# Late butterfly weights loaded group by group, outer weights and bias packed by partition, and the rows of ones written first

## The reference, cut to what matters

```python
def butterfly(y, weights, dim):
    for stage in range(weights.shape[0]):
        s = 2 ** stage
        nb = dim // (2 * s)
        yr = y.reshape(*lead, nb, 2, s)
        a, b = yr[..., 0, :], yr[..., 1, :]
        w = weights[stage].reshape(nb, s, 2, 2)
        na = w[..., 0, 0] * a + w[..., 0, 1] * b
        nb2 = w[..., 1, 0] * a + w[..., 1, 1] * b
        y = jnp.stack([na, nb2], axis=-2).reshape(*lead, dim)
    return y
...
h = jnp.einsum('bsd,dh->bsh', x, W_exp) + b_exp
h = butterfly(h, up_weights, D_HIDDEN)
h = jax.nn.gelu(h + up_bias, approximate=False)
h = butterfly(h, down_weights, D_HIDDEN)
y = jnp.einsum('bsh,hd->bsd', h, W_con) + b_con
return y + down_bias
...
x = x + 0.5 * ffn(layernorm(x))
x = x + attn(layernorm(x))
x = x + 0.5 * ffn(layernorm(x))
```

## Time and profile before

| | |
|---|---|
| median of 3 runs | 2010.09 us (2008.09 to 2011.85) |
| profiled execution, its own time | 2014.8 us |
| span of its trace | 2013.0 us |
| TensorE busy in the span | 1953.7 us (97%) |
| VectorE, ScalarE, GpSimd busy | 1675.2, 1362.5, 306.0 us |
| TensorE's mean granted clock | 0.991 of full speed |

### The profile page before, as it was taken

How to read it: one execution, slowest core, us unless ns; L and a number is a source line. 1 busy time by engine, 2 the same in 40 slices (tenths; PEclk the granted TensorE clock), 3 DMA queues, 4 the chain that set the end, 5 groups by cost and what they waited for, 6 DMA issues and landing times.

```text
span 2013.0 us, 58994 instructions
## 1 busy us (share of the span) xinstructions
PE 1953.7 (97%) x24312; PEld 1200.6 (60%) x24312; DVE 1675.2 (83%) x3622; ACT 1362.5 (68%) x1642; POOL 306.0 (15%) x736
## 2 busy tenths in 40 slices
PE   2899999999999999999999999999999999999999
PEld 2787777655555555555555555555555555569998
DVE  5745666599999999999999999999999999847663
ACT  4521222378888888888888888888888888884444
POOL 1200000011111111111111111111111111124444
PEclk8999999899999999999999999999999999999999
DMA  4221112121121111111111211112111111101110
GB/s 125 71 98 51 50 52 88 67 49 42 39 53 40 48 45 44 42 39 53 40 48 45 44 43 39 53 40 47 45 44 43 39 53 32 61 28 63 55 51 22
DMA packets 85736, 102.20 MB, mean 51 GB/s; under 512 B 19676, under 2 KB 48092, under 8 KB 85468
## 3 DMA queue, kind: packets, MB, share of 16 engines
q1 hardware_dynamic: 85048, 98.08, 17.5%
q10 hardware_dynamic: 420, 0.34, 0.1%
HBM read 68.46 MB, written 29.36 MB: 49 GB/s over the span
## 4 chain that ended last, share of the span: by engine, by line
PE 91%; DVE 3%; issue 2%; SPq 1%; ACT 1%; POOL 1%; DMA 1%; POOLq 0%; ACTq 0%; DVEq 0%
PE PS L1145 32%; PE PS L1272 32%; PE PS L1122 7%; PE PS L1092 6%; PE PS L1252 6%; PE PS L1331 4%; PE PS L1197 2%; PE PS L1116 1%; PE PS L1058 1%; SPq L382 1%; DMA V<-down_w 1%; ACT PG L707 1%; DVE OA L805 1%; POOL QT L573 0%; DVE OA L910 0%
## 5 line engine op out<-in xcount | busy, mean ns | idle before, releaser
L707 ACT ACTIVATE PG<-PS 128x1024 f32<-128x1024 f32 (+1 forms) x1152 | 1117.2, 978 | 235.4 <-PE PS L1252 175.9
L934 DVE TENSOR_REDUCE MXP<-PS 128x1 f32<-128x512 f32 x1792 | 1099.9, 684 | 23.3 <-PE PS L1145 23.2
L1252 PE MATMUL PS<-QT,KT 50*128 50x512 f32 (+1 forms) x2304 | 803.8, 435 | 0.2 <-issue 0.2
L1145 PE MATMUL PS<-KT,QT 48*128 48x512 f32 (+3 forms) x2304 | 798.7, 432 | 2.6 <-DVE MXP L934 2.3
L1272 PE MATMUL PS<-PG,VH 128*17 128x128 f32 x16896 | 728.8, 276 | 0.2
L1272 PEld LDWEIGHTS PS<-PG,VH 128*17 128x17 f32 x16896 | 401.1, 97 | 413.7 <-issue 364.6
L1145 PEld LDWEIGHTS PS<-KT,QT 48*128 48x128 f32 x2304 | 340.7, 185 | 252.4 <-issue 141.6
L1252 PEld LDWEIGHTS PS<-QT,KT 50*128 50x128 f32 x2304 | 335.6, 185 | 10.5 <-issue 10.1
L930 DVE CUSTOM_DVE_ANT_0 PS<-PS,MASK 128x128 f32<-128x128 f32 (+3 forms) x512 | 248.8, 505 | 72.8 <-PE PS L1145 67.0
L553 POOL TENSOR_SCALAR_AFFINE_SELECT PG<-PG 128x128 f32<-128x128 f32 x512 | 137.2, 295 | 998.1 <-ACT PG L707 997.8
L631 ACT ACTIVATE PG<-PS,GB 128x512 f32<-128x512 f32 x128 | 90.3, 707 | 167.7 <-PE PS L1092 167.7
(11 more groups left out here) (111 smaller groups left out, 1201.8 us busy)
## 6 DMA issues: line engine op xcount, KB each, us to landing
QT<-q_parts SPq DMA_DIRECT2D x256, 64.0 KB
KT<-k_parts SPq DMA_DIRECT2D x256, 64.0 KB
q_parts<-OA SPq DMA_DIRECT2D x16, 512.0 KB, 2.8
QT<-q_parts SPq DMA_DIRECT2D x256, 32.0 KB
k_parts<-OA SPq DMA_DIRECT2D x16, 512.0 KB, 4.5
KT<-k_parts SPq DMA_DIRECT2D x256, 32.0 KB
o_parts<-OS SPq DMA_DIRECT2D x128, 64.0 KB
OA<-o_parts SPq DMA_DIRECT2D x32, 256.0 KB
```

The costliest lines, as they stand in the source:

```text
L707: nc.scalar.activation(PB[n % 2][half][:, :, q0:TILE], PS[:, half * 1024:half * 1024 + 1024].rearrange("p (k q) -> p k q", k=2)[:, :, q0:T ...
L934: nc.vector.tensor_reduce(dst, bank(b), AX.X, ALU.max).then_inc(mx_red, 1)
L1145: mm(bank(4 + qs % 2 if b is None else b, w), q[0:SC, (BT * place(j) + qs) * P:(BT * place(j) + qs + 1) * P].bitcast(f32r), k[0:SC, c * TI ...
L1252: last = mm(PS[:, (2 * half + k) * 512 + q0:(2 * half + k + 1) * 512], kt[0:SM, kb * P:(kb + 1) * P].bitcast(f32r), qt[0:SM, place(j) * TI ...
```

## The change

Three things change; the arithmetic stays.

1. Stages 5 and 6 are loaded with one DMA for each row group: 4 DMAs of 32 partitions and 2 of 64 in place of one each. The waits count 4 or 2 times 16 for them.
2. The outer weights of both sides and the up bias are put into one array on the host, ordered by partition (128 rows of 104 floats), and loaded by one DMA that ScalarE issues after its inner stages. The three DMAs on SyncE's queue go away.
3. GpSimd fills the rows of ones before it builds the down product, and no longer between the end of `fold_down` and the first bias addition.

```diff
+        OUTER = sb("OUTER", [P, 2 * 48 + HB])
+        DU, DD = (OUTER[:, 48 * i:48 * (i + 1)].rearrange("p (s g e) -> p s g e", s=3, g=4) for i in range(2))
+        UB = OUTER[:, 96:96 + HB]
...
+        def inner_landed(s):
+            return 16 * (1 if 2 ** s < 32 else P // 2 ** s)
...
-            eng.wait_ge(loaded[0], 16)
+            eng.wait_ge(loaded[0], inner_landed(0))
...
-                eng.wait_ge(loaded[s], 16)
+                eng.wait_ge(loaded[s], inner_landed(s))
...
-            eng.dma_start(dst[:, w_offset(s):w_offset(s + 1)],
-                          rows.unsqueeze(1).to_broadcast([P // n, n, HB * 2 * n])).then_inc(sig, 16)
+            w = dst[:, w_offset(s):w_offset(s + 1)]
+            if n < 32:
+                eng.dma_start(w, rows.unsqueeze(1).to_broadcast([P // n, n, HB * 2 * n])).then_inc(sig, 16)
+            else:
+                for g in range(P // n):
+                    eng.dma_start(w[g * n:(g + 1) * n], rows[g:g + 1].to_broadcast([n, HB * 2 * n])).then_inc(sig, 16)
...
-            for w, d in ((up_w, DU), (down_w, DD)):
-                sp.dma_start(d[:, :, :, :], w[INNER:STAGES].rearrange("s (g p) e -> p s g e", p=P)).then_inc(in_d, 16)
-            sp.dma_start(UB[:, :], up_b).then_inc(in_d, 16)
...
+            pool.wait_ge(const_rdy, 2)
+            nc.gpsimd.memset(NK[NEXT // 2:NEXT, :], 1.0)
+            nc.gpsimd.memset(CK[NEXT // 2:NEXT, :], 1.0).then_inc(att_init, 1)
+            pool.wait_ge(att_init, 1)
             inner_product(nc.gpsimd, FD, link, in_down)
...
-            pool.wait_ge(md_ps, 4)
-            nc.gpsimd.memset(NK[NEXT // 2:NEXT, :], 1.0)
-            nc.gpsimd.memset(CK[NEXT // 2:NEXT, :], 1.0).then_inc(att_init, 1)
-            pool.wait_ge(att_init, 1)
             pool.wait_ge(ob_rdy, 1)
...
+            nc.scalar.dma_start(OUTER[:, :], outer).then_inc(in_d, 16)
...
-                    act.wait_ge(in_d, 48)
+                    act.wait_ge(in_d, 16)
...
-            dve.wait_ge(in_d, 48)
+            dve.wait_ge(in_d, 16)
```

More of the change, by code:

```diff
@@ L86, with program @@
 MU_ORDER = (0, 2, 1, 3)
-def program(nc, x, w_exp_t, up_w, up_b, down_w, w_con, b_con, down_b, wq, wk, wv, wo, out):
+def program(nc, x, w_exp_t, up_w, outer, down_w, w_con, b_con, down_b, wq, wk, wv, wo, out):
     ctx = ExitStack()
@@ L128, in program @@
         EXP_FIRST = sb("EXP_FIRST", [P, 1])
-        DU = sb("DU", [P, 3, 4, 4])
-        DD = sb("DD", [P, 3, 4, 4])
-        UB = sb("UB", [P, HB])
+        OUTER = sb("OUTER", [P, 2 * 48 + HB])
+        DU, DD = (OUTER[:, 48 * i:48 * (i + 1)].rearrange("p (s g e) -> p s g e", s=3, g=4) for i in range(2))
+        UB = OUTER[:, 96:96 + HB]
         GB = sb("GB", [P, HB])
@@ L941, in _ @@
                     dve.wait_ge(mix_v, 3 * HB)
-                    nc.vector.tensor_tensor(GB[:, :], T1[:, :, D], UB[:, :], ALU.add).then_inc(gb_rdy, 1)
+                    nc.vector.tensor_tensor(GB[:, :], T1[:, :, D], UB, ALU.add).then_inc(gb_rdy, 1)
                     dve.wait_ge(gb_rdy, 1)
@@ L1365, in by_partition, with outer_by_partition @@
                  for s in range(INNER)]
-        return np.concatenate([np.stack(inner), w[INNER:STAGES]])
+        return np.stack(inner)
+    def outer_by_partition(w):
+        w = np.asarray(w).reshape(STAGES, HID // 2, 4)[INNER:STAGES]
+        return w.reshape(STAGES - INNER, HID // (2 * P), P, 4).transpose(2, 0, 1, 3).reshape(P, -1)
     def heads_last(w):
@@ L1375 @@
         "up_w": by_partition(L0_ffn_up_weights),
-        "up_b": np.asarray(L0_ffn_up_bias).reshape(HB, P).T,
+        "outer": np.concatenate([outer_by_partition(L0_ffn_up_weights), outer_by_partition(L0_ffn_down_weights),
+                                 np.asarray(L0_ffn_up_bias).reshape(HB, P).T], axis=1),
         "down_w": by_partition(L0_ffn_down_weights),
```

## The result

The changed kernel takes 1999.79 us (median of 6 runs, 1998.03 to 2002.36), the kernel before 2009.28 us in the same comparison: a ratio of 0.9952 (0.9941 to 0.9963), or 9.5 us (7.4 to 11.9). The forecast was 1993.4, with a range of 1989 to 1998.5; faster was right, 16.7 us was too much, and the median lies 1.3 us outside the range. Two more sessions gave 0.9943 and 0.9948. Medians here and in the table are over all runs; the ratios compare means and leave out three disturbed runs, one of the bias later (whose median without it is 1997.36), one of OUTER alone and one of the kernel before in the session of the parts.

A forecast was written before the change was run, and what follows sets the result against it. A queue was taken to bound the start, TensorE the attention. An earlier chain (14.5 us) plus the ones (2.2) saves 16.7 us; 2010.1 - 16.7 = 1993.4 us, range 1989 to 1998.5.

The forecast's parts named there:

- What bounds the start: First 90 us: a queue, not an engine, sets the pace; stage 6 crawls on two DMA engines at 55 GB/s.
- the issue of DU, DD and UB: SyncE's queue, 4.14 to 22.83 us: dropping these three loads frees 18.7 us, so x is issued near 4.7.
- This rate is the open cost: Start loads: 0.79 MB of stages 5 and 6 at x's 354 GB/s take 2.2 us; tile 1 lands at 14.3.
- The rule on how many engines a transfer uses: Stages 5 and 6: largest number up to 16 dividing the slowest dimension; 64 or 32 rows outermost would use all 16.
- The rule against splitting: Stage loads: splitting into disjoint partition halves isn't worth it, as they share engines; by it alone 2005.0 us.
- The whole chain shifts by 14.5 us: Tile 1's statistics to TensorE's L1092: 18.7 us long, starting at 14.3 instead of 28.81, so L1092 starts at 33.0.
- The fold chain with 1.3 us to spare: ScalarE's four blocks, folded after `WE` lands, ready at 16.2, before the variance at 17.5.
- OUTER late: Rival at the start: packed load lands at 26.6, 5.8 us gained, 2004.3; chance 0.09 for 4 to 11 us gain.
- The ones: First residual, 69 to 79 us: early memsets cost nothing and close TensorE's gap, 2.2 us (1.5 to 2.4).
- The sum: Whole kernel: 14.5 us from the start plus 2.2 from the ones, 16.7 us saved.
- What it saves there should be kept to the end: After the start: attention, 600 to 1000 us, is TensorE-bound and untouched, so time saved in the first 90 us remains.

The follow-up runs named there:

- the bias later: Changed kernel, but GpSimd adds the bias to tile 0 only once VectorE has normalized tile 1; 1997.88 us, ratio 0.9929 to the kernel before.
- OUTER alone: Kernel before with only the packed outer weights and bias on ScalarE's queue, stage 6 still one DMA; 2008.95 us, ratio 0.9996.
- groups alone: Kernel before with only stages 5 and 6 loaded group by group, DU, DD and UB still on SyncE's queue; 2002.01 us, ratio 0.9972.
- Own rows in one DMA: Changed kernel, but host writes stage 5 and 6 rows once per partition, one 128-partition DMA per stage; 1996.22 us, ratio 0.9924 to the kernel before.
- own rows by group: Changed kernel with a row for each partition in stages 5 and 6, still DMAs of 32 and 64 partitions; 2000.72 us, ratio 0.9951 to the kernel before.
- The product behind the mixes: Changed kernel with GpSimd's down product after VectorE's 24 up mixes, and bias added after tile 1's normalization; 1993.40 us, ratio 0.9925 to the kernel before.
- the ones alone: Kernel before with only GpSimd's two memsets of ones moved early; 2007.63 us, ratio 0.9992.
- all three mends: Changed kernel with one-DMA per-partition rows for stages 5 and 6, down product after 24 up mixes, later bias; 1992.49 us, ratio 0.9917 to the kernel before.

## Why the forecast was too large, step by step

**What bounds the start: right.** A queue did, and the two nearly idle stretches were stage 6 on two engines. The parts alone show it: groups alone give most of the gain, and OUTER alone gives 0.6 us since the issue of x then stands for 13.84 us behind stage 6. Of the 18.7 us that the text put to the issue of DU, DD and UB, the 11.91 of DU were stage 6's doing.

**"This rate is the open cost" (354 GB/s for stages 5 and 6): the first step that failed.** It was taken from the stretch of x, in which each partition reads bytes of its own. The pieces ran at 211 to 283 GB/s, and `WE` landed at 12.80 where the sum has 11.2, the statistics of tile 1 2.2 us later than forecast (1.4 and 1.5 in the two repeats, so some 0.7 of it is scatter). The text looked for a broadcast's price in the number of engines alone. Own rows in one DMA gave 366 to 371 and `WE` at 11.25, own rows by group 231 to 279: the price is that of loading in pieces of 32 and 64 partitions. The rule on how many engines a transfer uses (the Trainium skill, page "DMA: Bandwidth & Descriptors", section "Why a DMA increments its semaphore by 16 and not by 1") held: share 1.05. The rule against splitting (same page, "Rules for kernel authors") was no reason against splitting a transfer that was on two engines to begin with: by it alone the time was to be 2005.0. But its advice, one transfer over 128 partitions, is what own rows in one DMA bore out.

**"The whole chain shifts by 14.5 us": the second step that failed.** The length of 18.7 us was read from a trace in which GpSimd's product lay partly elsewhere: its largest multiplication was at 43.71, beside the split. With the down stages landing 20 us sooner, all of it fell on the statistics, mixes and normalizations: 21.2 us. I had checked only whether the product would be in time for its reader, not whom it would lie beside. The trace of before had the sign of it already:

```profile
30.63 0.69 DVE L775 TENSOR_SCALAR MEAN<-LN 128x8 f32<-128x8 f32 x1
...
33.19 1.55 POOL L307 TENSOR_TENSOR V<-V 128x512 f32<-128x512 f32 x1 [1.90 <-DMA V<-down_w]
...
33.76 2.10 DVE L805 TENSOR_SCALAR XN<-X,MEAN,RSTD 128x256 f32<-128x256 f32 x4
...
63.98 1.38 DVE L805 TENSOR_SCALAR XN<-X,MEAN,RSTD 128x256 f32<-128x256 f32 x4
```

The four normalizations take 2.10 us beside GpSimd's 128x512 multiplication and 1.38 at 63.98, with GpSimd idle; L775 takes 0.69 and not 0.17 beside one of 128x256 at 30.57. So 1.2 of the 18.7 us were this wait too, and the undisturbed chain is 17.5 us. The product behind the mixes brought it to that, and normalizing without it didn't help while the mixes still had it. The Trainium skill has the rule, page "SBUF — State Buffer", section "SBUF: two separate sides": VectorE and GpSimd have one port pair in common, an exclusive lock for a whole instruction. The traces agree, 2.19 us for a 128x8 operation.

**The fold chain with 1.3 us to spare: right.** ScalarE waited 2.2 us for the variance. Nor was OUTER late: it landed near 11.7, 6.8 us after its issue at 4.92, ahead of ScalarE's first mix at 15.37.

**The ones: right that they cost nothing at the new place, wrong in what they free.** 2.2 us were forecast, with 1.5 as the lower bound; the first product of tile 1 against the transposes of `fold_down` moved by 11.71 - 10.97 = 0.74 us. The gap was to close because the bias is early; but early means beside the normalization of tile 1, which it stretched by 2.0 us. It is the same mechanism, and the bias later removed it. (A slip beside it changes nothing: by the text's own terms the bias would have ended 3.0 us before L1122 starts, not 2.)

**The sum.** 16.7 was forecast. Later loads take 2.2, the longer chain 2.5, the ones 1.5. The clock gave 1.2 back: it reached 1.00 sooner within tile 0's products, so that the transposes of `fold_down` came 10.97 us earlier and not 9.81. That makes 11.7 us at the start of tile 1, as the trace has it (85.58 - 73.87). The 1.2 us are luck of the two executions and no effect of the change: the same stretch, from the first product with `MU` to the transposes of `fold_down`, is 15.2 us in the one trace of before and 14.1 with OUTER alone and with the ones alone. Without them 10.5 us are left, near the medians' 9.5.

**"What it saves there should be kept to the end": nearly.** At the transposes of tile 5 for the attention the difference is 10.0 us, at the first scores of attention (388.88 and 380.09) 8.8. Part of the loss is a new wait:

```profile
PE PS L1150 <- DMA KT<-k_parts: 1.2, 1, 1.2
```

From the store of K for tile 3 to its read-back it was 5.45 us (211.09 to 216.54), before 3.66. Such a wait (0.4 to 1.8 us) is in ten of the eleven traces whose prologue is shorter by over 7 us, and not in the kernel before, with OUTER alone or with the ones alone; nor is it in the shortest prologue, that of all three mends, so a shorter prologue doesn't by itself bring it. Why the store is slower there was not tried and stays open. The other 1.2 us are the lower clock from 368 us on. The gain of the medians, 9.5 us, lies between these 8.8 us and the 11.7 at tile 1; with a clock that scatters runs by 4 us it can't be split further.

## What to carry to other kernels

When work on GpSimd moves in time, ask not only who waits for it but also which VectorE operations it will lie beside: here those with two operands in SBUF, and the normalization with its two scalars, stood until GpSimd's instruction was done, while those that read PSUM and the statistics (6 in 2.05 us) didn't feel it. A load whose pattern begins with a dimension of 2 moved 55 GB/s at a share of 0.14, and the issues behind it on the queue stood; look for such a share, and mend it with one DMA over all 128 partitions rather than with pieces (366 against 211 to 231 GB/s). And a single profiled execution can lie 5 us off the medians, as that of before did at a mean clock of 0.991; so compare places in the trace, not spans, and look at the clock there too.

## What the runs showed of the hardware that I had not expected

The DMA share is no measure of speed: it was 1.00 and 1.07 at 366 and 371 GB/s and 1.02 to 1.05 at 211 to 231, the latter with pieces of 32 and 64 partitions. Reading one row for many partitions costs nothing that shows: 211 and 283 GB/s against 231 and 279 with rows of their own. The issue of a DMA with 1536 pieces takes 0.58 us behind stage 6 in pieces and 11.91 behind stage 6 in one DMA on two engines; a second one behind it takes 5.21 either way. GpSimd's memsets of 32x4096 (3.5 us each) lay beside VectorE's multiplications of the up product and did not stretch them (0.42 us for 128x256, 0.43 before), unlike its operations that read SBUF.
